# Sum the two products of a step by an accumulating DMA, and a new order of the front

## The reference

```
# for each of 4 batches
xc    = causal_conv4(in_proj_w @ ctx^T)                     # 256 channels x 256 tokens
u     = silu(xc + conv_b)
dt, B, C = split(x_proj_w @ u)                              # 8, 16, 16 rows
delta = softplus(dt_proj_w @ dt + dt_proj_b)
A     = -exp(A_log)                                         # 256 x 16
state_n[t] = state_n[t-1] * exp(delta[t] * A_n) + delta[t] * u[t] * B_n[t]      # n = 0..15
y     = (sum over n of state_n * C_n + D * u) * silu(layernorm(x))
x2    = x + tanh(g_xattn) * y
# feed-forward on layernorm(x2): tokens rounded to 8 bits, weights to -1, 0, 1
h     = silu(q(x2) @ q(w_gate)) * (q(x2) @ q(w_up))         # 1024 wide
out   = x2 + tanh(g_ffn) * (q(hadamard(h)) @ q(w_down))
```

## Time and profile before

| | |
|---|---|
| runs | 221.14, 221.41, 222.14 us; median 221.41 |
| profiled execution | 220.58 us |
| its span, first to last instruction | 218.8 us |
| mean granted TensorE clock | 0.966 |
| PE busy | 188.9 us, 86% |
| DVE busy | 188.0 us, 86% |
| ACT busy | 168.9 us, 77% |
| POOL busy | 108.0 us, 49% |
| loads and stores | 5.05 MB read, 1.05 MB written, nearly all of the reading in the first 20 us |

### The profile page before, as it was taken

How to read it: one execution, slowest core, us unless ns; L and a number is a source line. 1 busy time by engine, 2 the same in 40 slices (tenths; PEclk the granted TensorE clock), 3 DMA queues, 4 the chain that set the end, 5 groups by cost and what they waited for, 6 DMA issues and landing times. The chain is left out here.

```text
span 218.8 us, 3665 instructions
## 1 busy us (share of the span) xinstructions
PE 188.9 (86%) x1221; PEld 152.7 (70%) x1228; DVE 188.0 (86%) x290; ACT 168.9 (77%) x298; POOL 108.0 (49%) x143
## 2 busy tenths in 40 slices
PE   2747889999899999899999999998998987686773
PEld 1534567887697998578989897797885776653751
DVE  1384938899999999998999999999989996889983
ACT  0278799999989969898967989993997811895373
POOL 1004700678708388029998991299920489510000
PEclk9965599999999999999999999999999999999998
DMA  5894000000000000000000000000000000000001
GB/s 135 264 343 182 0 1 4 0 0 0 3 0 0 3 1 1 0 3 0 1 3 0 0 3 24 1 27 0 0 0 3 25 0 27 0 0 0 27 24 48
DMA packets 8147, 6.33 MB, mean 29 GB/s; under 512 B 2202, under 2 KB 7874, under 8 KB 8130
## 3 DMA queue, kind: packets, MB, share of 16 engines
q1 hardware_dynamic: 6066, 6.01, 8.4%
q10 hardware_dynamic: 2064, 0.10, 0.6%
HBM read 5.05 MB, written 1.05 MB: 28 GB/s over the span
## 5 line engine op out<-in xcount | busy, mean ns | idle before, releaser
L1036 ACT ACTIVATE decay<-delta,zero_c,aneg 128x255 f32<-128x255 f32 x128 | 65.8, 588 | 1.6 <-DVE delta L1686 1.4
L1611 DVE TENSOR_TENSOR_SCAN state<-decay,BC 128x512 f32<-128x512 f32 x32 | 38.8, 1212 | 5.6 <-PE BC L397 3.8
L1611 DVE TENSOR_TENSOR_SCAN state<-decay,UP 128x512 f32<-128x512 f32 x32 | 38.4, 1201 | 1.1 <-issue 0.6
L1694 DVE TENSOR_TENSOR prod<-state,BC 128x1024 f32<-128x1024 f32 x32 | 38.4, 1200 | 0.7 <-PE BC L444 0.5
L1498 POOL TENSOR_TENSOR wnat<-wnat 128x512 f32<-128x512 f32 x18 | 22.9, 1275 | 26.2 <-DVE wnat L1738 25.4
L397 PE MATMUL BC<-diagB,duT 128*128 128x256 f32 x128 | 33.7, 386 | 0.7 <-DVE state L1611 0.5
L460 PE MATMUL PY<-id,prod 128*128 128x128 f32 x256 | 33.2, 273 | 1.1 <-DVE prod L1694 1.1
L397 PE MATMUL UP<-diagB,duT 128*128 128x256 f32 x128 | 33.3, 382 | 0.0
L460 PEld LDWEIGHTS PY<-id,prod 128*128 128x128 f32 x256 | 29.2, 141 | 3.9 <-DVE prod L1694 1.7
L397 PEld LDWEIGHTS BC<-diagB,duT 128*128 128x128 f32 x128 | 22.3, 190 | 5.2 <-issue 2.0
L397 PEld LDWEIGHTS UP<-diagB,duT 128*128 128x128 f32 x128 | 22.7, 190 | 3.6 <-issue 1.2
(11 more groups left out here) (250 smaller groups left out, 383.1 us busy)
## 6 DMA issues: line engine op xcount, KB each, us to landing
xs<-in_x_dram SPq DMA_DIRECT2D x1, 1024.0 KB, 8.8
wnat<-in_L_ffn_w_gate_dram SPq DMA_DIRECT2D x1, 1024.0 KB, 12.0
wnat<-in_L_ffn_w_up_dram SPq DMA_DIRECT2D x1, 1024.0 KB, 14.5
wnat<-in_L_ffn_w_down_dram SPq DMA_DIRECT2D x1, 1024.0 KB, 13.9
out_dram<-ot SPq DMA_DIRECT2D x8, 128.0 KB, 1.7
ctxs<-in_ctx_dram SPq DMA_DIRECT2D x1, 384.0 KB, 4.3
ctxs<-in_ctx_dram SPq DMA_DIRECT2D x1, 128.0 KB, 2.9
inw<-n_L_xattn_in_proj_w_dram SPq DMA_DIRECT2D x1, 128.0 KB, 2.6
```

Of the source, the lines that this page charges most:

```text
L1036: last = nc.scalar.activation(decay[:, m % RING, h, n, 1:L], delta[:, b % 2, h, 1:L], ACT.Exp, bias=zero_c[:], scale=aneg[:, h, NB * j + n ...
L1611: nc.vector.tensor_tensor_scan(state[:, g % STATES, h].rearrange("p n l -> p (n l)"), decay[:, g % RING, h].rearrange("p n l -> p (n l)"), ...
L1694: nc.vector.tensor_tensor(prod[:, g % RING].rearrange("p h n l -> p h (n l)"), state[:, g % STATES].rearrange("p h n l -> p h (n l)"), PC. ...
```

## The change

1. For g below `SUMMED` = 28 the two products of a step are added before TensorE sees them: GpSimd waits for `times_C(g)` and issues a DMA that adds the second state's half of the buffer to the first's, in place (128 partitions x 2 halves x 256 float32, 256 KB to be added). `accumulate(g)` waits for that DMA's semaphore and issues 4 transposes instead of 8. The last four steps stay as they were.
2. The loads of `dt_proj_b` (`dtb`) and of `D` (`dskip`) go from ScalarE's queue to SyncE's: `dtb` behind x and ahead of the three weights, `dskip` behind all loads. Each has a semaphore of its own.
3. TensorE gets products of ones by ones, `warm(i)` and `warm_later(i)`, two matmuls of 128 x 128 x 128 in float32 each, whose results nobody reads. There are 17 calls in the front: two around `setup_x_dbl`, one between `x_dbl(0)` and `dt_proj(0)`, 14 between `dt_proj(0)` and `first_B_T`.
4. All five orders are written anew. The front's are below; in the steps the calls shift against each other by a few places. In the tail `for_silu` stands ahead of `last_norm(0)` and both `last_norm` ahead of `inter_out(2, 1)`.

```diff
+SUMMED = B * STEPS - 4
...
+        pair_summed = [sem(f"pair_summed_{i}") for i in range(RING)]
...
             sp.dma_start(xs[:].rearrange("p b c d -> p (b c) d"), tiles(x)).then_inc(ld_x, 16)
+            with nc.allow_non_contiguous_dma(reason="one value per partition"):
+                sp.dma_start(dtb[:], dt_proj_b.rearrange("(h p) -> p h", p=P)).then_inc(ld_dtb, 16)
...
             sp.dma_start(had[:], hadamard).then_inc(ld_had, 16)
+            with nc.allow_non_contiguous_dma(reason="one value per partition"):
+                sp.dma_start(dskip[:], D.rearrange("(h p) -> p h", p=P)).then_inc(ld_D, 16)
...
+            def warm(i):
+                if i == 0:
+                    pe.wait_ge(consts, 1)
+                for n in range(2):
+                    nc.tensor.matmul(X[:, P * n:P * (n + 1)], onesf[:], onesf[:], start=True, stop=True)
...
+            def warm_later(i):
+                pe.wait_ge(act_setup, 2)
+                for n in range(2):
+                    nc.tensor.matmul(PB[:, P * n:P * (n + 1)], onesf[:], onesf[:], start=True, stop=True)
...
             def accumulate(g):
                 b, j = divmod(g, STEPS)
-                pe.wait_ge(dve_prod, g + 1)
+                if g < SUMMED:
+                    pe.wait_ge(pair_summed[g % RING], 16 * (g // RING + 1))
+                else:
+                    pe.wait_ge(dve_prod, g + 1)
...
                 for h in range(HALF):
-                    for n in range(NB):
+                    for n in range(1 if g < SUMMED else NB):
...
+            def pair_sum(g):
+                pool.wait_ge(dve_prod, g + 1)
+                nc.gpsimd.dma_start(prod[:, g % RING, :, 0], prod[:, g % RING, :, 1], accum_op=ALU.add
+                                    ).then_inc(pair_summed[g % RING], 16)
```

More of the change, by code:

```diff
@@ L729, in _ @@
             first_in_proj()
+            warm(0)
             setup_x_dbl()
+            warm(1)
             setup_dt()
             setup_in_proj()
-            setup_late()
-            x_dbl(0)
-            dt_proj(0)
+            x_dbl(0)
+            warm_later(0)
+            dt_proj(0)
+            warm(2)
+            warm_later(1)
+            warm(3)
+            warm(4)
+            warm_later(2)
+            setup_late()
+            warm(5)
+            warm(6)
+            warm(7)
+            warm(8)
+            warm(9)
+            warm(10)
+            warm_later(3)
+            warm_later(4)
+            warm(11)
             first_B_T()
             in_proj(1, 0)
-            C_rows(0)
             du_T(0)
@@ L747, in _ @@
             drive_rows(2, 0)
+            gate_T(0)
             drive_rows(2, 1)
-            accumulate(0)
-            C_rows(1)
             dt_proj(1)
@@ L970, in setup_loads @@
                 act.dma_start(alog[:], A_log.rearrange("(h p) n -> p h n", p=P)).then_inc(ld_gate, 16)
-                with nc.allow_non_contiguous_dma(reason="one value per partition"):
-                    for dst, src in ((dtb, dt_proj_b), (dskip, D)):
-                        act.dma_start(dst[:], src.rearrange("(h p) -> p h", p=P)).then_inc(ld_conv, 16)
                 nc.scalar.preload_act_table_set("silu_and_others")
@@ L1239, in _ @@
             xpw_out()
+            tanh_gates()
             dtw_out()
-            tanh_gates()
             silu_u(0)
-            inw_out()
-            ctx_out()
             for_exp()
             dt_rows(0)
+            inw_out()
             high_pieces(0)
-            first_rstd()
-            spread(0)
-            exp_A()
-            softplus(0)
-            copy_BT(0)
-            weight_abs(0)
+            spread(0)
+            softplus(0)
+            ctx_out()
+            weight_abs(0)
+            exp_A()
+            copy_BT(0)
+            first_rstd()
             decays(0, 0)
             decays(0, 1)
+            decays(1, 0)
+            copy_duT(0)
+            decays(1, 1)
             for_silu()
-            copy_duT(0)
+            silu_u(1)
             silu_z(0)
-            silu_u(1)
             for_exp()
-            decays(1, 0)
-            decays(1, 1)
             decays(2, 0)
-            decays(2, 1)
             dt_rows(1)
             copy_BT(1)
+            decays(2, 1)
+            high_pieces(1)
             decays(3, 0)
-            high_pieces(1)
+            spread(1)
             decays(3, 1)
-            spread(1)
             decays(4, 0)
@@ L1292, in _ @@
             copy_BT(2)
+            decays(9, 0)
             high_pieces(2)
-            decays(9, 0)
             decays(9, 1)
@@ L1326, in _ @@
             dt_rows(3)
-            copy_BT(3)
-            high_pieces(3)
             decays(17, 1)
@@ L1331, in _ @@
             decays(18, 1)
+            copy_BT(3)
+            high_pieces(3)
             decays(19, 0)
@@ L1542, in _ @@
             weight_scale(0)
+            pair_sum(3)
+            pair_sum(4)
             weight_scale(1)
+            pair_sum(5)
+            weight_scale(2)
+            pair_sum(6)
+            split(2)
+            pair_sum(7)
             diagonals(1, 2)
-            split(2)
+            pair_sum(8)
+            softplus_tail(2, pool, nc.gpsimd, pool_front_link, 0)
             diagonals(1, 3)
-            weight_scale(2)
-            softplus_tail(2, pool, nc.gpsimd, pool_front_link, 0)
@@ L1579, in _ @@
             second_rstd(2)
+            pair_sum(24)
             token_factors(2)
+            pair_sum(25)
+            pair_sum(26)
+            pair_sum(27)
+            diagonals(3, 3)
             fold_tile(2, 0, 0)
@@ L1911, in _ @@
             scan(6, 1)
+            weight_round(0)
             times_C(5)
@@ L1914, in _ @@
             scan(7, 1)
-            weight_round(0)
             weight_round(1)
+            times_C(6)
             weight_out(0)
-            times_C(6)
             scan(8, 0)
+            weight_out(1)
+            weight_round(2)
             scan(8, 1)
@@ L2000, in _ @@
             stats2(2, dve_ln_link)
+            times_C(25)
             absmax2(1, 0)
-            times_C(25)
             scan(27, 0)
-            round_down(1, 0)
             scan(27, 1)
             times_C(26)
+            round_down(1, 0)
+            scan(28, 0)
             token_scale(2, dve_ln_link)
@@ L2009, in _ @@
             round_tokens(2)
-            scan(28, 0)
-            round_down(1, 1)
             scan(28, 1)
             times_C(27)
+            round_down(1, 1)
             scan(29, 0)
```

359 lines of the change are left out of this document (188 added, 171 removed).

## The result

The changed kernel took 233.22 us (median of 4 runs, 231.80 to 236.01) against 221.27 for the kernel before (4 runs, 220.17 to 222.14): ratio 1.052, 95% interval 1.046 to 1.059. Slower, by 12 us; my forecast was 223.9, my range ended at 230.

The account below looks back on a forecast made before the run. VectorE was taken to bound the steps, ScalarE 31.7 to 53.6 us, dependency chains both ends. Step 6 +3.0, relief and waits 0, tail -0.5 made +2.5 us: 223.9 us median, range 217.5 to 230.

Parts of the forecast that it names:

- (a): Steps: 4 transposes fewer in 28 steps save TensorE 12.3 us, returning half of VectorE's 4.2 us idle time, 2.1 us.
- (b): Price of a pair sum on GpSimd: 1.0 us to issue, 3.0 us to landing.
- (c): Steps: what waits for the sums, at full GpSimd and batch ends, loses 2.2 us; bounds 0 and 8 us.
- the ring: Steps: product buffers come back four steps later, over 15 us, so 4 us of issue and landing is covered.
- (d): Front until u: taps gain 3.2 us, lost as tanh waits for alog; u at 14.8 us against 14.93.
- (e): Front: TensorE's clock falls between 11 and 15 us; 14 pairs of ones follow dt_proj(0), copy_BT ends at 28.8 us.
- (f): Front from copy_BT through ScalarE's work to the first scan: it starts at 34.4 us, 2.7 us later.
- (g): ScalarE's stretch to step 6: one table load more, one decay group less, +0.3 us; step 6 begins 3.0 us late.
- (h): Tail: the table load ahead of hT moves to where ScalarE waits, last_norm(1) comes ahead of hT; -0.5 us.
- 2: Rival: GpSimd is the bound at 2 us an issue, VectorE waits some 6 us more; 230 us, chance 0.16.
- 4: Rival: a sum's issue stands still during VectorE's one-input passes over SBUF; +1 us, 225 us, chance 0.03.

Follow-up runs that it names:

- f: Kernel before, in its own orders, transposing only the first product of steps 0 to 27; 220.78 us, ratio 0.998.
- o: Changed kernel with the sums of steps 3, 4, 5, 9 and 10 made by GpSimd's own adds instead of DMAs; 226.11 us, ratio 1.021.
- p: Kernel before plus the 28 DMA sums, each placed in GpSimd's queue where its product is ready; 270.67 us, ratio 1.221.
- k: Changed kernel with the sums of steps 5, 9 and 10 made by GpSimd's own adds instead of DMAs; 231.72 us, ratio 1.044.
- h: As e, but GpSimd issues the 28 DMAs on scratch memory, two in flight, and nobody else waits for them; 233.65 us, ratio 1.049.
- b: Changed kernel with all 28 sums made by GpSimd's own add instead of the DMA; 224.47 us, ratio 1.009.
- c: Changed kernel with its DMAs on scratch memory, each waiting for the one before, and all 8 transposes; 250.50 us, ratio 1.127.
- e: Changed kernel without any sum, transposing only the first product of steps 0 to 27; 224.71 us, ratio 1.015.
- g: Changed kernel with GpSimd's weight_scale(2) and diagonals(2, 1) held until VectorE's weight_round(1) and round_tokens(0) are done; 230.57 us, ratio not used.
- a: Changed kernel without any pair sum, with all 8 transposes again; 229.63 us, ratio 1.033.

## Why the prediction was wrong

**(a) TensorE's relief, 2.1 us of at most 4.2.** The bound was right, the value was 0 in the old orders (f). I also misread the price of a transpose: sixteen in 1.91 or 1.95 us are 0.12 each, not 0.11; TensorE's busy time fell by 8.7 us (f), where I had 12.3. Neither moves the sum.

**(b) Price of a sum.** Issue 1.21 us (taken 1.0), landing 3.7 (taken 3.0): right, both inside their bounds. GpSimd's busy time grew by 33.9 us. The estimate of 2.6 us for a landing, by the Trainium skill's page "DMA: Bandwidth & Descriptors", section "Anatomy of one DMA — SWDGE (gpsimd) path", is 1.1 short for this accumulating DMA.

**(c) What waits for it: 2.2 us, and (a) + (c) = 0. This is the step that failed.** From step 1 to step 31 it is 8.8 us. What I named did happen: `residual(0)` waited 1.48 us (1.3 predicted), and `inter_T(0, 1)` waited 1.42 us for the fold (1.7 predicted).

```profile
79.47 0.70 DVE L1772 TENSOR_TENSOR PY<-PY,szT 128x512 f32<-128x512 f32 x1 [1.48 <-PE PY L492]
```

 What I did not price is VectorE waiting for GpSimd. I took VectorE's 144 us as given because its instructions stay the same, and asked only who is late for it. Two of its passes took 5.6 us longer (4.24 and 3.00 instead of 1.21 and 0.42), TensorE stood 4.2 and 2.2 us behind them and came back at half clock. Five adds in place of five DMAs take 6.1 of the 8.8 away (o). I also wrote that "4 us of issue and landing is covered by the ring". The ring covers the buffer, not TensorE's queue: in p, with `accumulate` where it was, TensorE waited 37.1 us for landings.

**(d) Front, until `u`.** `tanh` still waited for `alog`, `u` was ready at 14.0 instead of 14.8, as `alog` landed 0.8 us earlier. Right in kind.

**(e), (f) The clock and the products of ones.** The clock fell where I said, at about 13.7 us. I took it as back behind the first pair of ones after `dt_proj(0)`, at 20.8 us. No run shows that point: it came back at 17.2 here. My reading of the rise before was also off: TensorE had been at work without a break since the start of `dt_proj(0)` at 18.46, not since its end. In this front the rise is not one number: in kernels whose queues are the same up to there it came back at 16.4 (k), 16.6 (h), 17.2 (after), 21.9 (b), 22.1 (c), 23.2 (e) and 23.7 (g), and never fell in a and o. Where it came back at 23.2 (e), the first scan started at 34.45 us; I had 34.4. That is right in the chain and lucky in the number: `dt_proj(0)` ended at 19.1 there instead of my 19.9, and the clock came back 2.4 us later than I had it. In the changed kernel's profile the scan started at 31.49. The profile before (back at 26.4) could not tell that there are other cases.

```profile
13.00:14.00 1.00, 0.00 (x0) 0.00 (x0) 1.00 (x5) 0.97 (x3) 0.00 (x0) 0.87 1.09 384
14.00:17.00 3.00, 2.94 (x9) 2.24 (x9) 0.95 (x9) 2.13 (x4) 0.00 (x0) 0.50 1.10 367
17.00:18.00 1.00, 1.00 (x4) 0.66 (x4) 0.24 (x2) 1.00 (x3) 0.00 (x0) 0.92 1.03 385
```

**(g) Step 6 late by 3.0 us.** It was 0.6 late (54.23 against 53.58), since the 2.7 of the front did not come in this run. ScalarE's stretch grew by 0.8 where I had 0.3; `times_C(1)` is 2.0 us late there, as `C_rows(1)` now comes behind `drive_rows(3, 1)`, and catches up most of it by step 2 (0.8 late).

**(h) Tail -0.5.** It is 0.5 us longer from step 31 on: within what one run can tell, but no gain.

**Rivals.** 2 (GpSimd the bound, 230) was nearest in time, and the chain of waits looks like it; of its signs, GpSimd was full for long stretches, while VectorE was idle 7.5 us after step 6, not more than 8. b refutes it, since the same load on GpSimd as adds costs about 9 us less. 4 looked at the right pair of engines and had the sides reversed: not the sum waits for VectorE, VectorE waits for GpSimd. The Trainium skill's page "SBUF — State Buffer", section "Who interferes with whom", allows both for VectorE's two-port modes: whoever issues first holds the shared ports and the other is blocked. The rows of o agree: the pass waited for the add under way, and `weight_scale(2)` became longer behind it. I read the rule for the sums only, and priced it at 1 us and 0.03. With a DMA in the run the pass stands not for one operation of GpSimd but to the end of the run: g, k and o show it here.

**What the 12 us are.** In the profiled executions (11.2 us, the parts rounded): 2.0 up to step 1, 8.8 from step 1 to 31, 0.5 behind it. Of the 8.8, the new orders with halved transposes are -1.5 (e), 28 sums as adds +2.3 (b), and the DMAs in their place +8.0, of which 6.1 go with five of them (o). Each is a difference of two single profiles. What the remaining 1.9 are was not taken apart; the wait for landings is at most 0.9 of them (h).

## What to carry to other kernels

An engine's busy time is not fixed by its instruction list: before giving GpSimd more work, and DMAs above all, find the one-input passes of VectorE over SBUF that will run beside it, and where a DMA is in GpSimd's unbroken run, price each up to the end of that run. A wait for a DMA costs what stands behind it in the waiting engine's queue, so the consumer has to be moved before the producer is changed. If the time per step matters, take it between fixed steps: the medians here were blurred by a clock in the front that comes back at different times.
